# Zero fills of the expert regions issued by ScalarE, and SyncE's early order changed

## The reference, cut to what matters

```python
x = x + tanh(g_xattn) * cross_attention(layernorm(x), ctx, ctx, ...)   # 8 batches, 256 x 512, 16 heads, rotary
x = x + tanh(g_ffn) * routed_moe(layernorm(x), ...)

def _routed_moe(x, gate_w, w0, w1, wo):          # 2048 tokens, 8 experts, 2 of them for each token
    top_logits, top_idx = jax.lax.top_k(logits, K)
    top_w = jax.nn.softmax(top_logits, axis=-1)
    for e in range(E):
        h = jax.nn.silu(x @ w0[e]) * (x @ w1[e])
        out = out + cw[:, e:e + 1] * (h @ wo[e])
```

## Time and profile before

| | us |
|---|---|
| median of 3 runs | 1104.04 (1103.65 to 1109.77) |
| the profiled execution | 1105.53 |
| its span, first to last instruction | 1103.6 |

### The profile page before, as it was taken

One profiled execution on the slowest core, in us unless ns is written; L12 is line 12 of the kernel. 1 busy time (PEld: TensorE's weight loads), 2 busy tenths in 40 slices (PEclk: granted clock), 3 DMA queues, 4 the chain that ended last, 5 costly groups with the idle time before them and its releaser, 6 DMA issues. The chain is left out here.

```text
span 1103.6 us, 18854 instructions
## 1 busy us (share of the span) xinstructions
PE 1048.4 (95%) x5894; PEld 425.6 (39%) x5894; DVE 805.8 (73%) x1619; ACT 672.1 (61%) x921; POOL 383.4 (35%) x491
## 2 busy tenths in 40 slices
PE   8998998989999999998987999999999999999997
PEld 3322233333333333232343444444444444444443
DVE  7886798998988898889786756757467475755632
ACT  2286787777777787788754656647247564644421
POOL 4672755848485774611142111011111111011101
PEclk9998999999999999999999999999999999999999
DMA  6346635323234323215256865867558575864333
GB/s 204 120 110 167 201 111 176 120 91 119 83 116 137 117 81 107 78 68 174 96 165 198 225 159 140 211 146 181 123 131 219 112 197 124 220 154 77 61 57 48
DMA packets 182223, 149.65 MB, mean 136 GB/s; under 512 B 122672, under 2 KB 144176, under 8 KB 182128
## 3 DMA queue, kind: packets, MB, share of 16 engines
q1 hardware_dynamic: 170432, 126.06, 40.7%
q0 software_dynamic: 7456, 17.57, 7.9%
q10 hardware_dynamic: 4240, 4.84, 1.5%
HBM read 73.80 MB, written 40.28 MB: 103 GB/s over the span
## 5 line engine op out<-in xcount | busy, mean ns | idle before, releaser
L1502 PE MATMUL psum<-W,xs 128*128 128x512 f16 x1824 | 398.2, 380 | 6.9 <-DVE xs L1708 3.9
L601 ACT ACTIVATE W<-psum,es 128x512 f32<-128x512 f32 x512 | 321.8, 688 | 69.8 <-PE psum L363 68.0
L845 DVE TENSOR_REDUCE MX<-psum 128x2 f32<-128x1024 f32 x256 | 308.5, 1218 | 45.9 <-PE psum L351 44.5
L1502 PEld LDWEIGHTS psum<-W,xs 128*128 128x128 f16 x1824 | 177.3, 98 | 226.3 <-issue 8.8
L363 PE MATMUL psum<-stg 50*128 50x512 f16 x512 | 171.0, 388 | 12.5 <-ACT W L601 9.6
L1776 POOL DMA_INDIRECT out<-xs,target x34 | 53.1, 1563 | 279.8 <-ACT xs L700 279.4
L351 PE MATMUL psum<-stg 48*128 48x512 f16 x512 | 145.7, 385 | 2.8 <-DVE MX L845 2.8
L1632 DVE TENSOR_TENSOR xs<-xs,psum 128x512 f32<-128x512 f32 x68 | 46.3, 685 | 131.0 <-ACT xs L685 130.9
L376 PE MATMUL psum<-W 128*32 128x512 f32 x1024 | 138.5, 613 | 0.0
L685 ACT ACTIVATE xs<-psum,i 128x512 f32<-128x512 f32 x68 | 46.1, 681 | 133.6 <-PE psum L1502 106.4
L726 DVE SCALAR_TENSOR_TENSOR W<-stg,scw,W 128x1024 f16<-128x1024 f32 x96 | 117.3, 1279 | 9.1 <-ACT W L712 8.9
(11 more groups left out here) (243 smaller groups left out, 1175.3 us busy)
## 6 DMA issues: line engine op xcount, KB each, us to landing
stg<-in_w SPq DMA_DIRECT2D x16, 2048.0 KB, 8.2
stg<-in_wo SPq DMA_DIRECT2D x7, 2048.0 KB, 10.1
stg<-scr SPq DMA_DIRECT2D x186, 64.0 KB, 2.3
Xs<-zero SPq DMA_DIRECT2D x33, 264.0 KB, 3.3
scr<-W SPq DMA_DIRECT2D x32, 256.0 KB, 3.2
W<-W SPq DMA_DIRECT2D x60, 128.0 KB, 2.2
xs<-in_x SPq DMA_DIRECT2D x8, 512.0 KB, 4.0
out<-xs SPq DMA_DIRECT2D x8, 512.0 KB, 3.5
```

The costliest lines, as they stand in the source:

```text
L601: act.activation(m.Pb[:, c % 2, hh, :], m.psT[tile % 2], ACT.Exp, scale=m.es[:, hb // 2:hb // 2 + 1]).then_inc(S["exped"], 1)
L845: dve.tensor_reduce(m.MX[:, hb % 2, c0:c0 + 9:8], m.psS[tile % 2], AX_X, ALU.max, negate=True).then_inc(S["maxed"], 1)
L1502: return pe.matmul(out, rows, m.wh[(e % 2, w)][:, wp, cols], start=start, stop=stop)
```

## The change

ScalarE issues the fills, one transfer of 512 rows for each of the 8 experts, with the blank tile read four times over. Three stand in phase -1 (steps 3, 8, 13), five in phase 0 (steps 1, 4, 7, 10, 13). VectorE writes the token number at step 1 of phase -1 instead of step 13, and POOL waits for 8 transfers instead of 32. SP has no fills; swap(0, 4) and max_rows(3) come ahead of the loop, and so ahead of the stacking of half-batch 3.

```diff
+def fill_rows(eng, m, S, e):
+    eng.wait_ge(S["zeroed"], 1)
+    dst = m.Xs[e * REG:e * REG + 128 * LEAST, :].rearrange("(t p) n -> p t n", p=128)
+    blank = m.zero[:, :].rearrange("p (t n) -> p t n", t=1).to_broadcast([128, LEAST, ROW])
+    eng.dma_start(dst, blank).then_inc(S["filled"], 16)
...
+FILLED_AT = {(-1, 3): 0, (-1, 8): 1, (-1, 13): 2, (0, 1): 3, (0, 4): 4, (0, 7): 5, (0, 10): 6, (0, 13): 7}
...
 # scalar_attention, in the loop over steps
+                if (ph, s) in FILLED_AT:
+                    fill_rows(act, m, S, FILLED_AT[(ph, s)])
...
 # vector_attention, spread
-        if ph == -1 and s == 13:
+        if ph == -1 and s == 1:
             dve.wait_ge(S["router"], 16 * 7)
...
 # pool_attention, scatter
-        pool.wait_ge(S["filled"], 16 * NE * LEAST)
+        pool.wait_ge(S["filled"], 16 * NE)
...
 # sync_attention
-    def fill_rows(n):
-        sp.wait_ge(S["zeroed"], 1)
-        for i in range(n, n + 4):
-            r = i // LEAST * REG + i % LEAST * 128
-            sp.dma_start(m.Xs[r:r + 128, :], m.zero[:, :]).then_inc(S["filled"], 16)
...
     keep(1, 3)
-    fill_rows(0)
-    fill_rows(4)
     load_ctx(sp, m, S, io, 3)
+    swap(0, 4)
+    max_rows(3)
     for ph in range(1, NH):
...
-        if a < NH:
+        if 1 < ph and a < NH:
             swap(0, a)
-        max_rows(2 * ph + 1)
+        if 1 < ph:
+            max_rows(2 * ph + 1)
...
-        if ph < 4:
-            fill_rows(8 * ph)
...
-        if ph < 4:
-            fill_rows(8 * ph + 4)
```

## The result

| us | before | after |
|---|---|---|
| median of 12 runs | 1103.85 (1101.10 to 1109.77) | 1108.58 (1104.52 to 1113.02) |
| ratio to before | | 1.0040 (95%: 1.0026 to 1.0054) |
| the profiled execution | 1105.53 | 1105.20 |
| its span | 1103.6 | 1103.3 |

The change costs 4.7 us where 4.9 us of gain were forecast. It is a change within 1%, but its median lies outside the range of 1096.5 to 1106.0.

The account below looks back on a forecast made before the run. TensorE, 95% busy, was taken as the bound, losing time mainly in phase 1 to late rows of maxima and a slow clock. Gains of 6.2 us less costs of 1.1, 0 and 0.2 gave 4.9: 1104.04 to 1099.1 us, range 1096.5 to 1106.0.

Parts of the forecast that it names:

- Gains 1 to 3: Phase 1's middle: 2.37 us stall and 2.3 us of slow clock gone; phase 2's start: 0.47 us of idling gone.
- Gain 1: Middle of phase 1: TensorE's 2.37 us stall goes, as SP issues max_rows(3) ahead of the stacking.
- Gains 4 and 5: Phase 4's start: 0.5 us of idling gone; phase 3: 0.6 us, POOL's rope coming sooner.
- Cost 1: Phase 1's start: SP's transfers for half-batch 2 late among the early fills, 1.1 us, bounds 0 to 4.4.
- Cost 2: Phase 0's start: 2.7 us of slack covers the delay by three fills; 0 lost, upper bound 1.0.
- Costs 3 and 4: ScalarE's fill issues between phase 0's exponentials, 0.2 us, at most 2.0; VectorE's moved copy and POOL's wait, none.
- R2: Phase 0: ScalarE's issues push the exponentials out, costing 2.0 us; 1100.9 us; chance 0.10.
- R1: Before phase 1: ScalarE's fills starve SP, tile 7.4 us late plus 2.3 of slow clock; 1107.5 us; chance 0.12.
- R3: Stall and slow clock move to phase 1's start, phases 3 and 4 give nothing; near 1103.2 us; chance 0.13.
- R4: Middle of phase 1: the tile at 97.88 waited for something else, so no gain; 1104 us; chance 0.02.

Follow-up runs that it names:

- fills_late: Kernel after with ScalarE's eight fills moved to steps 1, 4, 7, 10 of phases 1 and 3; 1098.53 us, 0.9948 of before.
- order_only: Kernel before with only SP's new order, swap(0, 4) and max_rows(3) ahead of stacking half-batch 3, all 32 fills still on SP; 1099.57 us, 0.9954.
- late_old_order: Kernel after with ScalarE's eight fills in phases 1 and 3 and SP's order as in the kernel before; 1098.04 us, 0.9958 of before.
- far_later: Kernel after with SP's far_write(2) and far_read(2) behind the rows of maxima, VectorE using them at phase 1's step 9, not 4; 1105.18 us, 1.0023.
- three_early: Kernel after with phase -1's three fills kept and phase 0's five moved to phases 1 and 3; 1101.84 us, 0.9988 of before.
- after_again: Second profile of the unchanged kernel after; this execution took 1107.9 us.
- after_again2: Third profile of the unchanged kernel after; this execution took 1105.03 us.
- five_early: Kernel after with phase 0's five fills kept and phase -1's three moved to phases 1 and 3; 1104.01 us, 1.0011 of before.

## Why the prediction was wrong, by its own steps

**Gains 1 to 3: right.** Worked at 2.37 + 2.3 + 0.47 = 5.1 us, all of them in phase 1's length; fills_late, where nothing disturbs them, shows 34.7 to 29.25, 5.5 us. In the kernel after 2.0 us of this are eaten by the moved slow clock. Gain 1's reason was one of two that suffice: order_only has it by the order, late_old_order by the fills' absence.

**Gains 4 and 5: right in size.** 1.1 us forecast; phase 3 fell by 1.1 in fills_late, by 1.6 in the kernel after, and by 0.1 in order_only.

**Cost 1: the step that failed.** It took 1.1 us with an upper bound of 4.4; measured are 5.71 us of idling and 2.0 of slow clock. Two things were mis-sized. The first is the delay along the chain keep, stacking, rows, which the fills make without the far write: the prediction counted 1.6 of slack and 1.6 + 1.1 of delay, the 1.1 without a row behind it, but the twelve stackings also hold SP's queue for 8.44 us in far_later (8.86 in the kernel after), where they took 5.99 in the kernel before, so that the rows' issue is late too. That part is 2.4 us by far_later. The second is what the prediction left out: the far write, 128 rows of 4 bytes into DRAM, stood in SP's timeline before as well, and landed 8.4 us after its issue at 64.53. Its neighbours were slow there too: keep(1, 2), issued at 63.27, landed after 7.6 us, and keep(1, 1), issued at 40.83, after 2.4. With fills behind it everything queued stops for some 4 us. That part is 3.3 us. The upper bound was too low because it took as the worst neighbour a large load, which the trace had, and no small write. The slow clock was named in the rival but not put in the term. The forecast's own range was also drawn too narrow: its upper end, about 1101.5, follows from no sum, as the upper bounds of the costs together (4.4 + 1.0 + 2.0 against 6.2 gained) give 1105.2. Even that is 3.3 us under the median.

**Cost 2: failed.** 0 taken, upper bound 1.0; idle times of 1.1 to 4.6 us at phase 0's start, and 3.3 us by three_early's median. The slack of 2.7 us was real, but the three fills ahead were weighed by the landing of stackings among SP's own fills (3.8 us) and not by the row that the prediction itself cited for the rival: in 582:584 SP's queue has no packet beside ScalarE's transfer. The one packet between 40.1 and 41.6 us is the same. keep(1, 1) landed after 2.4 us in the kernel before, after 4.3 in the kernel after and after 5.6 in after_again, behind the second fill.

**Costs 3 and 4: right.** The eight issues take 0.38 to 0.40 us each and stand inside exponentials or evacuations; ScalarE's busy time in phase 0 is 22.08 us, as before (22.07). R2 is out.

**The rivals.** R1, at 0.12, is nearest to what happened: its price, 9.7 lost against 6.2, comes out at 10.0 lost (the kernel after against fills_late) for 5.1 gained (fills_late against before), and its time, 1107.5, is 1.1 us from the median. Its place was right, its account (three fills of 3.0 one after the other, 7.4 us late) was not: the tile idled 5.71 us, 3.3 of them by the far write, and R1 had nothing at phase 0's start, where 1.8 us are lost by the profiles and 3.3 by three_early's median. That its sum comes so near is luck. R3 was half right: the slow clock did fall at phase 1's start instead of the middle. R4 is out.

The Trainium skill's rule (DMA: Bandwidth & Descriptors, section on queues, rings and completion order), that an engine takes turns between queues, a packet at a time, was read in the prediction as at most half the bandwidth lost, which put the forecast 0.6 us lower still. The stretch 40.1 to 41.6 us does not agree with that reading: 282 packets of one queue to 1 of the other. Nor is it what the section says: its packet is a whole run of descriptors, typically about 9 to 17 and at most 64, while a packet of the profile is here one row of 2112 bytes. The 282 are, evenly spread, some 18 for each of the 16 engines, and the 512 rows of a whole fill are 32, so the rule by itself allows such a stretch. In 75:89, with both queues loaded, they share (2346 packets to 1292, 2.58 to 2.63 MB); what decides between the two pictures is not shown by any run here.

**Open.** In the kernel before, and in order_only, the clock is also at 0.50 for 6.8 us early in phase 13 (from 464.0 and 458.5 us), and this phase takes 31.9 us; in the kernel after the fall is half as long (phase 13: 30.4), and in the kernels with late fills there is none (29.9). These 2 us are in no step, and are part of what lies between the profiles of before and of the kernels with late fills; whether they are in the medians is not known. None of TensorE's idle times ahead of it is longer than 0.9, and no run was made for it.

## What to carry to other kernels

Moving the fills to another issuing engine freed SP's queue (6.46 us for the first eight), and no transfer time: where a chain of small transfers (stack, swap, row) has 2 us of slack, a 1 MB fill that takes all 16 engines for an estimated 3.2 us (1.08 MB at the 341 GB/s of the earlier trace rows) must not stand in front of it. Put bulk work where the chain has room, as fills_late and late_old_order do (0.9948 and 0.9958 of before, both better than either kernel given). In fills_late the rows for phase 1's second half are issued to 88.46 and their tile comes at 94.61, 6.1 us later, with two fills in flight behind their issue. Judge a quiet phase by this slack and not by its average DMA share of 0.35. When two edits each remove the same wait, test each alone: here the removal of fills was enough, the order was enough as well (0.9954), and the two together brought no more that the intervals show.

## What the runs showed of the chip that was not expected

A write of 128 rows of 4 bytes to DRAM took 9.8 us to landing in the kernel after, 8.5 in far_later and 7.5 to 9.9 in the kernel before, and transfers of every queue nearly cease behind it (11 GB/s in 70.60:74.50 with fills queued, 44 GB/s in 83:92 of far_later with loads queued); in the kernel before, with no fill near, the transfers beside it were slowed as well (keep(1, 2) to 7.6 us, the swap of 66.97 to 5.3 where that of 61.99 took 2.8), but no tile waited for them. The Trainium skill (DMA: Bandwidth & Descriptors, Specifications) says that transfers under 512 bytes are done by read-modify-write; and its section on back-pressure in remote DMA, which is about transfers between cores and not about this case, says that stalled writes also stall the engine's other queues. The stop of both queues looks like the second; no run here separates the size of the rows from their target, so the cause of the stop stays open.

ScalarE's fill shut SP's queue out for 1.5 us (1 packet to 282) and for 1.3 us (0 to 240) where SP's transfers were issued inside it. A reduction over partitions on GpSimd, 0.38 us in its own row, came with some 6 us of standstill ahead of it and 7 behind it, though an indirect DMA of GpSimd started 0.30 us behind that of 216.00. TensorE's clock of 0.50 (1.2 GHz) lasted 6.8 us each time in phases 0 and 1 and cost phase 1 some 1.5 to 2.0 us (31.3, 31.0, 30.8 and 30.7 in the kernel after, after_again2, after_again and five_early, 29.25 and 29.0 without); it came behind idle times of 2.39 and 5.71 us at phase 1's start and of 3.69 and 4.62 at phase 0's.
